# Attention products in blocks of two pairs, scores two steps ahead, and the sums of the weights 250 columns wide

## What is computed

```python
xn = _ln(x, norm_s_w, norm_s_b)
spatial_out = _spatial_experts(xn, idx_s, ...)     # attention, 8 heads of 64
xt = _ln(x, norm_t_w, norm_t_b)
temporal_out = _temporal_experts(xt, idx_t, ...)   # causal attention, 8 heads
fused = _cross_mha(spatial_out, temporal_out, ...) # attention, 8 heads
x = x + fused
x = x + gelu(_ln(x) @ mlp_w1.T + mlp_b1) @ mlp_w2.T + mlp_b2
```

## Time and profile before

| | |
|---|---|
| runs | 1907.59, 1907.62, 1909.65 us, median 1907.62 |
| profiled execution | 1907.21 us, its span 1905.4 us |
| TensorE matmuls busy | 1702.3 us (89%) |
| VectorE busy | 1256.8 us (66%) |
| ScalarE busy | 713.1 us (37%) |
| GpSimd busy | 667.1 us (35%) |
| DMA | 58.09 MB, mean 30 GB/s |
| granted TensorE clock | 0.958 of full speed, mean |

### The profile page before, as it was taken

How to read it: one execution, slowest core, us unless ns; L and a number is a source line. 1 busy time by engine, 2 the same in 40 slices (tenths; PEclk the granted TensorE clock), 3 DMA queues, 4 the chain that set the end, 5 groups by cost and what they waited for, 6 DMA issues and landing times.

```text
span 1905.4 us, 32421 instructions
## 1 busy us (share of the span) xinstructions
PE 1702.3 (89%) x10735; PEld 1377.4 (72%) x10735; DVE 1256.8 (66%) x2481; ACT 713.1 (37%) x1346; POOL 667.1 (35%) x615
## 2 busy tenths in 40 slices
PE   2999988876999999988899988989999998799998
PEld 1788656756778777767777876877777775597896
DVE  7678668884767666755666765666767677774332
ACT  1223211024755444545455543354555453120110
POOL 3213001002546353342423226133333367374440
PEclk9899999987999999989999999999999999899999
DMA  3101000011031000020000000000000002111111
GB/s 112 34 7 45 12 10 24 12 60 40 7 125 46 28 12 7 7 120 12 12 12 12 7 1 18 23 12 12 6 12 7 7 1 83 38 61 45 45 34 54
DMA packets 24791, 58.09 MB, mean 30 GB/s; under 512 B 2537, under 2 KB 4805, under 8 KB 24013
## 3 DMA queue, kind: packets, MB, share of 16 engines
q1 hardware_dynamic: 24650, 56.18, 8.9%
HBM read 44.87 MB, written 11.30 MB: 29 GB/s over the span
## 4 chain that ended last, share of the span: by engine, by line
PE 39%; DVE 8%; issue 2%; POOL 2%; ACT 1%; DMA 0%; DVEq 0%; SPq 0%; POOLq 0%; ACTq 0%
PE ps L2434 7%; PE ps L2250 7%; PE ps L2366 6%; PE ps L2463 4%; PE ps L2347 4%; PE ps L2308 3%; PE ps L2351 3%; DVE max_part L1770 2%; DVE feat L1804 2%; PE ps L2388 2%; DVE p_sum L1793 1%; PE ps L2377 1%; POOL p_sum L1054 1%; DVE tok_z L1882 1%; PE ps L2319 0%
## 5 line engine op out<-in xcount | busy, mean ns | idle before, releaser
L1770 DVE TENSOR_REDUCE max_part<-ps 125x2 f32<-125x500 f32 x520 | 329.2, 673 | 124.9 <-PE ps L2308 116.4
L1349 ACT ACTIVATE p_raw<-ps 125x500 f32<-125x500 f32 x520 | 297.3, 585 | 290.0 <-PE ps L2351 281.9
L2366 PE MATMUL ps<-p_raw,v_rows 125*64 125x250 f32 x2080 | 285.4, 396 | 9.4 <-ACT p_raw L1349 7.3
L1054 POOL TENSOR_TENSOR p_sum<-p_sum,p_raw 125x500 f32<-125x500 f32 x144 | 192.6, 1337 | 221.9 <-ACT p_raw L1349 221.4
L2366 PEld LDWEIGHTS ps<-p_raw,v_rows 125*64 125x64 f32 x2080 | 129.2, 139 | 91.6 <-ACT p_raw L1349 20.5
L1793 DVE TENSOR_TENSOR p_sum<-p_sum,p_raw 125x500 f32<-125x500 f32 x144 | 115.6, 803 | 101.4 <-ACT p_raw L1349 99.1
L1610 DVE TENSOR_SCALAR onehot<-iota_h,win_key,key_t 125x320 f16 x453 | 176.4, 389 | 0.5 <-issue 0.5
L1054 POOL TENSOR_TENSOR p_sum<-p_raw 125x500 f32<-125x500 f32 x56 | 71.3, 1274 | 293.0 <-PE ps L2377 238.0
L2347 PEld LDWEIGHTS ps<-q_both_b,k_both_b 128*125 128x125 f32 x520 | 99.0, 190 | 100.6 <-issue 85.6
L2250 PE MATMUL ps<-xa_hi,w_hi 128*128 128x418 f32 (+1 forms) x448 | 151.5, 338 | 19.9 <-POOL w_lo L922 8.9
L2347 PE MATMUL ps<-q_both_b,k_both_b 128*125 128x250 f32 x520 | 164.1, 336 | 0.0
(11 more groups left out here) (398 smaller groups left out, 3847.0 us busy)
## 6 DMA issues: line engine op xcount, KB each, us to landing
w_raw<-in_w_mlp SPq DMA_DIRECT2D x32, 256.0 KB, 2.6
w_raw<-in_w_gps SPq DMA_DIRECT2D x16, 256.0 KB, 2.6
w_raw<-in_w_tp SPq DMA_DIRECT2D x16, 256.0 KB, 2.5
w_raw<-in_w_sp SPq DMA_DIRECT2D x12, 256.0 KB, 2.5
w_raw<-in_w_cr SPq DMA_DIRECT2D x12, 256.0 KB, 2.5
d_xt<-xb_hi SPq DMA_DIRECT2D x1, 2508.0 KB, 7.4
d_xt<-xb_lo SPq DMA_DIRECT2D x1, 2508.0 KB, 15.0
xa_hi<-d_xt SPq DMA_DIRECT2D x1, 2508.0 KB, 9.4
```

Of the source, the lines that this page charges most:

```text
L1054: pool.tensor_tensor(p_sum[:, 0, :], before, p_raw[:, g % PR, :], ALU.add).then_inc(s_add_a, 1)
L1349: act.activation(p_raw[:, g % PR, :], ps[0:TOK, g % 2, 0:4 * TOK], ACT.Exp, scale=SCALE).then_inc(s_exp, 1)
L1770: dve.tensor_reduce(part[:, y, :, j], ps[0:TOK, bank, 0:4 * TOK].rearrange("p (h k) -> p h k", h=2), AX.X, ALU.max)\
L2366: ins = pe.matmul(ps[r, bank, 0:2 * TOK], v_rows[:, n % 2, kt, h, :], p_raw[:, (g - 1 + h) % PR, cols], start=(b == 0 and x == 0), stop=last)
```

## The change

Scores run two steps ahead (LEAD = 2). Products are issued in blocks of up to two pairs at the end of a block's last step; a block ends earlier where the next pair would open a unit whose bank is still held by an output two units back. The denominator of a unit that ended in one block stands at the end of the next block, and VectorE's unit_out stands at that step. The sums are 250 wide: block 0 adds its two halves, each later block adds its two halves one after the other, into one of two sets of p_sum by the unit's parity. The due steps of side tasks are one step earlier.

```diff
-LEAD = 1
+LEAD = 2
...
+def product_blocks():
+
+    blocks, den_at, open_units = [], {}, []
+    for first, end in ((0, FIRST[8, 0]), (FIRST[8, 0], len(STEP))):
+        pairs = list(range(first + 1, end, 2))
+        while pairs:
+            block = [pairs.pop(0)]
+            while pairs and len(block) < BLOCK_PAIRS:
+                n, i, b, _ = STEP[pairs[0]]
+                if b == 0 and unit_of(pairs[0]) - 2 in open_units + [unit_of(g) for g in block]:
+                    break
+                block.append(pairs.pop(0))
+            dens, open_units = open_units, [unit_of(g) for g in block if g == LAST[STEP[g][0], STEP[g][1]]]
+            if not pairs:
+                dens, open_units = dens + open_units, []
+            blocks.append((block, dens))
+            for u in dens:
+                den_at[u] = block[-1]
+    return blocks, den_at
+
+BLOCK_PAIRS = 2
+BLOCKS, DEN_AT = product_blocks()
+BLOCK_END = {block[-1]: (block, dens) for block, dens in BLOCKS}
+PRODUCT_AT = {g: block[-1] for block, _ in BLOCKS for g in block}
...
-            due["R", n, i] = gf - 4
+            due["R", n, i] = gf - 5
             for x, task in enumerate(tasks):
-                due[task] = gf - 6 - 2 * (len(tasks) - 1 - x) // 3
-            due["Q", n, i] = gf - 9 - 2 * len(tasks) // 3
+                due[task] = gf - 7 - 2 * (len(tasks) - 1 - x) // 3
+            due["Q", n, i] = gf - 10 - 2 * len(tasks) // 3
...
             steps += SIDE[g]
-            n, i, b, h = STEP[g]
-            if h == 1:
-                steps.append(("P", g))
-                if b == 0 and g - 1 > first:
-                    steps.append(("D", 5 * n + i - 1))
-        steps.append(("D", 5 * STEP[end - 1][0] + 4))
+            if g in BLOCK_END:
+                block, dens = BLOCK_END[g]
+                steps += [("P", x) for x in block] + [("D", u) for u in dens]
...
-        p_sum = sb("p_sum", [TOK, 2, 4 * TOK], F32)
+        p_sum = sb("p_sum", [TOK, 2, 2, 2 * TOK], F32)
...
             def add_second_head(g):
...
+                u, done = 5 * n + i, ADD_NO[n, i, b]
+                total = p_sum[:, u % 2, 1, :]
+                halves = [p_raw[:, g % PR, 2 * TOK * x:2 * TOK * (x + 1)] for x in range(2)]
                 dve.wait_ge(s_exp, g + 1)
-                if b == min(1, blocks - 1):
-                    dve.wait_ge(s_den, 5 * n + i)
...
+                if b == 0:
+                    if u >= 2:
+                        dve.wait_ge(s_den, u - 1)
+                    dve.tensor_tensor(total, halves[0], halves[1], ALU.add).then_inc(s_add_b, 1)
+                else:
+                    dve.wait_ge(s_add_b, done - 2)
+                    dve.tensor_tensor(total, total, halves[0], ALU.add).then_inc(s_add_b, 1)
+                    dve.wait_ge(s_add_b, done - 1)
+                    dve.tensor_tensor(total, total, halves[1], ALU.add).then_inc(s_add_b, 1)
...
-            OUT_AT = {LAST[n, i] + 3: 5 * n + i for n in range(PASSES) for i in range(5) if (n, i) not in ((7, 4), (11, 4))}
...
-                    if g in OUT_AT:
-                        unit_out(OUT_AT[g])
+                    if g in BLOCK_END:
+                        for u in BLOCK_END[g][1]:
+                            unit_out(u)
```

More of the change, by code:

```diff
@@ L146, with unit_of @@
 LAST = {(n, i): STEP_NO[n, i, blocks_in(n, i) - 1, 1] for n in range(PASSES) for i in range(5)}
[L149 to L150 removed]
+def unit_of(g):
+    n, i, _, _ = STEP[g]
+    return 5 * n + i
+def product_blocks():
[20 more added lines that the diff above has]
+PRODUCT_AT = {g: block[-1] for block, _ in BLOCKS for g in block}
+ADDED = [(n, i, b) for n in range(PASSES) for i in range(5) for b in range(blocks_in(n, i))]
+ADD_NO = {(n, i, b): 2 * x + 2 - (5 * n + i + 1) for x, (n, i, b) in enumerate(ADDED)}
 def maxima(n, i):
@@ L1045, in add_first_head @@
                 n, i, b, _ = STEP[g]
-                blocks = blocks_in(n, i)
+                u, done = 5 * n + i, ADD_NO[n, i, b]
+                total = p_sum[:, u % 2, 0, :]
+                halves = [p_raw[:, g % PR, 2 * TOK * x:2 * TOK * (x + 1)] for x in range(2)]
                 pool.wait_ge(s_exp, g + 1)
-                if b == min(1, blocks - 1):
[L1049 to L1059, removed]
+                if b == 0:
+                    if u >= 2:
+                        pool.wait_ge(s_den, u - 1)
+                    pool.tensor_tensor(total, halves[0], halves[1], ALU.add).then_inc(s_add_a, 1)
+                else:
+                    pool.wait_ge(s_add_a, done - 2)
+                    pool.tensor_tensor(total, total, halves[0], ALU.add).then_inc(s_add_a, 1)
+                    pool.wait_ge(s_add_a, done - 1)
+                    pool.tensor_tensor(total, total, halves[1], ALU.add).then_inc(s_add_a, 1)
             for g in range(len(STEP)):
@@ L1784, in add_second_head @@
                 n, i, b, _ = STEP[g]
-                blocks = blocks_in(n, i)
+                u, done = 5 * n + i, ADD_NO[n, i, b]
+                total = p_sum[:, u % 2, 1, :]
+                halves = [p_raw[:, g % PR, 2 * TOK * x:2 * TOK * (x + 1)] for x in range(2)]
                 dve.wait_ge(s_exp, g + 1)
-                if b == min(1, blocks - 1):
-                    dve.wait_ge(s_den, 5 * n + i)
[L1789 to L1797, removed]
-                    dve.tensor_tensor(p_sum[:, 1, 0:2 * TOK], total[:, 0:2 * TOK], total[:, 2 * TOK:4 * TOK], ALU.add).then_inc(s_add_b, 1)
+                if b == 0:
+                    if u >= 2:
+                        dve.wait_ge(s_den, u - 1)
+                    dve.tensor_tensor(total, halves[0], halves[1], ALU.add).then_inc(s_add_b, 1)
+                else:
+                    dve.wait_ge(s_add_b, done - 2)
+                    dve.tensor_tensor(total, total, halves[0], ALU.add).then_inc(s_add_b, 1)
+                    dve.wait_ge(s_add_b, done - 1)
+                    dve.tensor_tensor(total, total, halves[1], ALU.add).then_inc(s_add_b, 1)
             def unit_out(u):
@@ L1885, in _ @@
                     last_out(task)
-                unit_out(unit_of(end - 1))
             for p in range(3):
@@ L2373, in denominator @@
                 bank = 2 + u % 2
-                pe.wait_ge(s_add_a, ADD_NO[n, i, blocks_in(n, i)])
-                pe.wait_ge(s_add_b, ADD_NO[n, i, blocks_in(n, i)])
+                pe.wait_ge(s_add_a, ADD_NO[n, i, blocks_in(n, i) - 1])
+                pe.wait_ge(s_add_b, ADD_NO[n, i, blocks_in(n, i) - 1])
                 for h, r in enumerate(HALF):
-                    ins = pe.matmul(ps[r, bank, 2 * TOK:4 * TOK], ones_f[:, :], p_sum[:, h, 0:2 * TOK], start=True, stop=True)
+                    ins = pe.matmul(ps[r, bank, 2 * TOK:4 * TOK], ones_f[:, :], p_sum[:, u % 2, h, :], start=True, stop=True)
                 ins.then_inc(s_den, 1)
```

7 lines of the change are left out of this document (2 added, 5 removed).

## The result

The changed kernel takes 1892.85 us (median of 4 runs, 1892.61 to 1893.07) against 1908.63 for the kernel before in the same comparison: ratio 0.9916, 95% interval 0.9899 to 0.9933, so 16 us less. The direction was forecast; the size was not. 34 us were forecast, and the measured gain is less than half of it.

What follows compares the result with a forecast made beforehand. TensorE's queue was taken to set attention's pace, VectorE in 14% of the stretch. Gains of 31, 20 and 12 us less costs of 4, 8, 4, 5, 6 and 3 gave -33 us: 1874 us, range 1845 to 1908.

Steps and rivals of the forecast that it cites:

- Switches: TensorE in attention: 128 fewer product groups at 0.28 us each; gain 31 us, bounds 0 and 51.
- Output's place: VectorE: unit output moved to the next block's end cuts turned-maxima waits; gain 20 us, bounds 0 to 30.
- Scores: TensorE: products stop waiting for exponentials, scores wait instead, an even exchange; plus 4 us for late ScalarE, bounds -7 and +16.
- Queries to maxima: Without product between, first maximum behind a query linear waits for ScalarE's and VectorE's copies; +8 us, bounds 0 and 13.
- R to the first score: Four causal units have only one score's 0.47 us between turned maxima and first score; +4 us, bounds 0 and 6.
- Banks: Maxima's banks reused with under 2.5 us of TensorE work between go from 64 to 124; +5 us, bounds 0 and 12.
- Sums: 250-wide sums add 200 instructions on VectorE, 32 to 70 us, 14% of it on the chain; +6 us.
- VectorE at the block's end: VectorE stands at the unit's output about 0.9 us longer in 56 units, covered by unissued maxima; +3 us, bounds 0 and 50.
- rival C: Slower: VectorE's queue at a block's end delays the next steps' maxima; +31 us, 1939 us, chance 0.10.
- Nothing: Two p_sum sets, GpSimd's weight splits, loads on SP's queue and the raw scores' ring were taken to cost nothing.
- B: VectorE's 70 us of extra work turns TensorE's saving into waits; about -8 us, 1900 us, chance 0.08.
- D: TensorE's gaps belong to each product's own start, not the switch, so blocks save nothing; 1905 us, chance 0.07.

Runs made afterwards that it cites:

- e12: Changed kernel with blocks of one pair and denominators ahead of the step's side tasks instead of behind the products: 1883.76 us, ratio 0.9858 to the kernel before.
- e4: Kernel before with each unit's output one step later on VectorE: 1906.67 us, ratio 0.9985.
- e11: Kernel before with each unit's output one step earlier on VectorE, at the step of its denominator: 1886.00 us, ratio 0.9890.
- e9: Kernel before with only the due steps of side tasks one earlier: 1902.86 us, ratio 0.9964.
- e1: Changed kernel with blocks of one pair instead of two, output still at the block's end: 1877.88 us, ratio 0.9841 to the kernel before.
- e7: Changed kernel with blocks of one pair and the output one step behind the block's end: 1895.29 us, ratio 0.9927 to the kernel before.
- e2: Kernel before with only the 250-wide sums on both engines and two sets of p_sum: 1910.38 us, ratio 1.0005.
- e5: Changed kernel, blocks of two pairs, with the unit's output one step behind the block's end: 1882.96 us, ratio 0.9866 to the kernel before.
- e10: Changed kernel with blocks of one pair and GpSimd's final bias additions held until VectorE's last sum: 1871.16 us, ratio 0.9800 to the kernel before.
- e16: Changed kernel, blocks of two, with each unit's reciprocal replaced by writing a constant, leaving out the division: 1863.49 us, ratio 0.9757 to the kernel before.
- e17: Changed kernel with blocks of one pair and each unit's reciprocal replaced by writing a constant: 1848.36 us, ratio 0.9681 to the kernel before.
- e15: Changed kernel, blocks of two, output one step later and GpSimd's bias additions held until VectorE's last sum: 1880.34 us, ratio 0.9848 to the kernel before.
- e13: One of a pair of runs with shorter maxima; the text describes it no further and gives no measured time.
- e14: The other of the pair of runs with shorter maxima; the text describes it no further and gives no measured time.

## Why the prediction was wrong

By its own terms:

1. **Switches** (forecast 31, from 128 x 0.28). The mechanism holds and was undersized. A switch costs 0.34 to 0.35 us by these rows: 0.09 in, 0.16 out, 0.10 for the second wide matmul; 43 us in the table. The 0.09 out came from comparing eight products before a score with eight before a denominator, which itself ran late; groups of 8 and 16 give 0.16. The Trainium skill, in "TensorEngine Tiling (Array Packing)", Key Properties, says that a change of tiling mode drains TensorE. The trace agrees: e12 adds 48 such changes and back without adding work, and each costs 0.31 us. I took off 14% for VectorE's share of the chain; the table shows that the loss has to be looked for place by place.
2. **Output's place** (forecast 20). R's wait fell as argued, by 27 to 30 us, but the time was not gained by the place. The place moved from three steps behind the unit's last step to four or six. Moved to four in the kernel before (e4), it takes R's wait to 17.2 us and gives 2 us, since the wait goes to the products; in the changed kernel it goes to the maxima (term 9). So this term came out near its lower bound, "the lateness appears elsewhere". The 21 to 24 us of e11 belong to the opposite move. And the due steps, one earlier in the same change, have no term in the sum at all: alone they halve R's wait and give 7 us (e9).
3. **Clock** (forecast 12): 5, by the table.
4. **Scores** (forecast +4 and an even exchange). The scores' side was counted rightly, 16 us, of which 12.9 were measured; the products' side was not, since 17 us by the rule were 7.3 in the waits (13 in the sorting). What I did not see is that the +16 belongs to the blocks and not to the lead: with single blocks it is nil (0.2 us in e1 and e7).
5. **Queries to maxima** (forecast +8): 13 us more.
6. **R to the first score** (forecast +4): 10 us more, 12.1 in seven waits where two made 1.8. The price was wrong: up to 2.6 us each, since in the row at 905.70 key copies and an exponential stand ahead of the rows on ScalarE, not the bare 0.74 us of two copies. Of this, 8.0 us stand in e1 too, so most of it is not of the blocks.
7. **Banks** (forecast +5): 22.7 instead of 9.1 us, so +14. The 6.0 us that the term started from are a row of the linears (L2250), which wait for banks that maxima filled; the maxima's own waits were 3.1 us and are left out there.
8. **Sums** (forecast +6): within the noise (e2). VectorE's 45 us more lie beside other waits in the kernel before; in the changed order they were not tried. The Trainium skill, in "VectorE: DVE Perf Modes", The TRN2 errata, speaks of a fixed latency for each instruction. VectorE's own time agrees (0.420 us for half the columns of 0.680); the run's time does not show it.
9. **VectorE at the block's end** (forecast +3): 10 (e5). This is the term that I called covered "by the maxima not yet being issued". What stood behind the output were the lower parts of the queries, and the first maximum behind them was already next in TensorE's queue (the row at 565.28). It is rival C's mechanism at a small price.
10. **Nothing** held for the weight splits and loads. It did not hold for the end of attention, which I never priced: the last denominator's wait rose by 4.4 us (8.4 before, 12.8 after) while the projection behind it waits 4.8 us as before (5.0). GpSimd's additions make most of it (e10). Why it rose is open: e11 ends earlier than the changed kernel and its wait is 8.5 us.

The step that failed is what comes back. The gains that terms 1 to 3 name were 63 us by forecast and 78 in the table. Terms 4 to 7 and 9 were +24 together, and the products' own wait was taken as paid for by term 4; measured, the waits of scores, maxima, linears and the short ones make +76, against which 13 for products stands. Of the 76, 66 are gone in e1, which takes back the blocks and with them the output's later place. Two parts of this are traced. Four scores and their side tasks follow each other without a product, so that ScalarE has less time between two users of a bank: that is shown for the scores, whose waits are 32 to 35 us with blocks of two (the changed kernel, e5, e16) and 10 to 11 with blocks of one (e1, e7, e17). And the output stands later and in front of the queries' lower parts: that is 10 us (e5). The rest is not attributed. That the lack of a product makes the maxima late by itself is not shown; with the output one step behind the block's end in both, their waits are 3 us apart (e5, e7).

Most signs listed under "Right" came true: the products' wait gone, the scores' 12.9 us, R's 10.9, the first maxima's 28.1, the clock 0.98. They test the mechanisms and say nothing of the size of the sum.

Of the rivals, B (1900) and C have a part of the mechanism, VectorE behind the gap and at the block's end, each too large. D is out: sixteen product matmuls in one group take 1.84 us and not twice 1.00, and the gap goes with the group (e12).

By runs: the output at the denominator's step is worth 21 to 24 us by itself (e11) and the due steps 7 (e9). With scores two ahead and the 250-wide sums beside them the whole is 31 (e1), so the scores' lead adds little if the parts add up, which was not tried one by one. What blocks of two do to the time has no single number: at the block's end they lose 15 us (e1), one step later they gain 12 (e7 against e5), each at its better place they lose 5, within the intervals, and with the tail mended 9 (e15 against e10).

What stays open is why e1's place gives so much: 12 of the 19 us between its stretch and e7's are work at half clock, and what in the order makes TensorE's clock fall less often was not taken apart. e13 and e14, the same pair with shorter maxima, gave no time.

## What to carry to other kernels

A product of narrow matmuls between two users of a bank is not only work: it is the time in which the other engines finish. Before grouping equal work to save switches, count for each consumer how much other work stands between it and its producer in the new list, and price every shortage, not the mean. And before rewriting an order, try each single position in it: one instruction pair moved by one step gave here at least what the rewriting gave. Last, compare two orders at more than one place of what stands beside them: e1 alone says that blocks of two lose 15 us, e7 beside e5 that they gain 12.

## What was not expected of the hardware

- VectorE's sum with both inputs in SBUF takes 0.42 us alone and 1.36 to 1.47 us while GpSimd runs its 1.4 us additions, at 1605.75 us for instance. In e10, with GpSimd held back, it takes 0.41 to 0.42.
- One step in VectorE's order moves TensorE's clock: e7 and e1 differ in the place of one output, the granted clock of the profiled executions is 0.959 and 0.969, and by the sorting above 12 of the 19 us between their stretches are work at half clock.
